# A four-layer transformer beside a two-of-eight expert layer: phases written out, tail and gathers reordered, new slot tables

## The chip, the cores and the metric

The kernel runs on one core of a Trainium2 chip. The metric is the time of one execution on the device in microseconds (us). Five engines work beside each other, each through its own list of instructions in order: PE (TensorE, matrix products), DVE (VectorE), ACT (ScalarE), POOL (GpSimd) and SP (SyncE, which here only starts transfers). They meet at semaphores: an instruction waits until a counter has reached a value, and what stands behind it in the same list waits too.

## The reference, cut to what matters

The input x has 2 rows of 1024 positions and 128 features. After one layer normalisation it goes through two things, whose results are both added to x:

```python
xn = layernorm(x)
x + attn(xn) + moe(xn)

# attn: 4 layers, 16 heads of 8 features, hidden width 512
mask = -inf above the diagonal, slope[h] * (k - q) below it
for i in range(4):
    x = x + mha(layer_norm(x, ln1), mask)      # softmax(q k / sqrt(8) + mask) v, then out_proj
    x = x + gelu(layer_norm(x, ln2) @ ffn1 + b1) @ ffn2 + b2
return layer_norm(x, final)

# moe: 8 experts of width 512; each position takes its two best, weighted by a softmax of the two logits
```

A softmax does not depend on which number is subtracted from a row of scores before the exponential, as long as the same number is used in numerator and sum.

## The kernel before, in words

Everything is written engine by engine, with all waits by hand. The work of attention is cut into 32 passes (U in the code): a pass is one layer, one row and a group of four heads. Four passes are a phase; there are eight phases, alternating between the two rows: an even phase does the attention of row 0 and the dense work of row 1, an odd one the other way round. Phase 0 is written out ("first"), phases 1 to 6 are three turns of a hardware loop (`Fori`) whose body holds an odd phase and an even one, and phase 7 is written out again ("last"). Behind phase 7 comes a tail (`END`) that finishes row 1: output projection, feed-forward and last normalisation, for two halves c = 0 and 1 of 512 positions.

In a pass each engine does two things at once. For the next pass, PE computes scores (L967, with the mask added by L972) and DVE takes their maxima (L1216, L1223); there are 40 such steps, through two banks of PSUM. For the present pass, PE computes the transposed scores with the maximum subtracted (L984, L990) in 24 slots, ACT takes the exponentials (L797), and PE multiplies by the values (L1002). POOL splits each maximum into three bf16 parts (`max_parts`, L601 to L608), PE transposes them (`turn`, L879), ACT copies them out (L766), and SP puts them as three rows into the operand of the transposed scores (`minus_max`, L455), for two halves of the positions. So `turn` must follow the end of a pass's maxima, and slot 0 or 8 of the pass follows `turn`.

Between the slots PE does the dense work, all through bank 7: output projection (`wo`, L938), normalised rows transposed (`ln1`, `ln2`, L887), hidden layer (`h`, L907 for attention's, L911 for the experts'), second layer (`y`, L924, L927), and `q`, `k`, `v` of the next layer (L948, L952). The order is written in tables, `PLANS`: `pace` says how many of the 40 score steps stand in each half slot (48 for each of four passes), `contents` gives the slot (0 to 95 in the phase) at which PE does a piece and the half slot at which another engine takes it out, and the rest are slots for ACT's gelu and splits and for DVE's statistics, reciprocals, normalisation and final step. A `turn` for half 1 takes the pass to which its slot belongs (slots 0 to 23 are pass 0, and so on).

The experts' rows are scattered by POOL in phase 0 (L614, 32 indirect transfers), and gathered back in phase 7 (`gather`, L641, 32 indirect transfers: 16 at the end of pass 0 and 16 at the end of pass 1, before the reciprocal roots `rstd_of`, L572, that stand behind them). In pass 2 POOL then weights and adds them (`combine`, L650, L654); DVE's `final` (L1210) needs these sums.

`wait_apart` (L373) is a wait in an instruction of its own, made so by a count on a semaphore that nobody reads (`passed`, L376).

In the tail before, PE's order is `wo` 0, `ln2` 0, four `h` of half 0, `wo` 1, `ln2` 1, four `h` of half 1, `y` 0, `y` 1. DVE copies the hidden layer out of PSUM (L1138) and computes the reciprocals and the normalisation for `wo` 1 (L1194, L1199) after the four `h` of half 0.

Of the kernel before, what the change touches and what calls it, by code (L numbers as in the profile page):

```python
# [57 lines left out]
def first_pass():  # L58

    steps = []  # L60
    for i in range(TB):
        for c in range(1 + i // 4):
# [12 lines left out]
        pace=("011111011111011111011111011111011101021111011111",  # L75
              "011111011111011112011110011111010111111111011021",
              "011111011111011112001111011111011111101111101111",
              "011101111001111100013101000043011111110111101111"),
        contents=(
# [6 lines left out]
        gelu=(14, 23, 59, 83), stats2=(1, 17), stats1=(19, 36),  # L86
        recip=(87, 5), norm=(94, 13), hi=(32, 45), mid=(36, 49), final=(72, 75)),
    "odd": dict(
        pace=("020111011110111111011110111110111111000311101111",
              "000103211020111101101001211111110111002111011102",  # L90
              "001021012011100121011110000430111101110120110012",
              "011101012111011011101110005310001011101111110102"),
        contents=(
# [11 lines left out]
        gelu=(13, 26, 59, 83), stats2=(2, 14), stats1=(21, 36),  # L105
        recip=(88, 8), norm=(95, 13), hi=(32, 45), mid=(36, 49), final=(73, 73)),
    "even": dict(
        pace=("011110111110101111101111111112011002011111012110",
              "000002321200111101111011110211010111101101111111",
              "001011112111011111111012011010011111210110011103",  # L110
              "101101220011101210010010100431111100110111011102"),
        contents=(
# [10 lines left out]
        gelu=(13, 27, 62, 85), stats2=(1, 14), stats1=(19, 36),  # L123
# [100 lines left out]
def build(nc, x, cA, rA, cB, moe1, moe2, router_w, rb, fin, ident, identb, iota, m1, m2, route, kcon, qcon, out):  # L224
    with ExitStack() as ctx:
# [147 lines left out]
        def wait_apart(eng, semaphore, value):  # L373

            eng.wait_ge(semaphore, value)
            eng.sem_inc(passed, 1)  # L376
# [1106 lines left out]
```

## Time and profile before

| | |
|---|---|
| median of 3 runs | 1548.06 us (1546.43 to 1549.83) |
| the profiled execution's own time | 1548.17 us |
| its span, first to last instruction | 1546.4 us |
| executed instructions in the profile | 35310 |
| PE busy | 1272.3 us (82%) |
| DVE busy | 997.0 us (64%) |
| ACT busy | 873.0 us (56%) |
| POOL busy | 379.2 us (25%) |
| mean granted clock of TensorE | 0.921 |

Times inside the profile are counted from the first instruction of the span. The profiled execution lies 1.8 us outside its span. "Idle before, releaser" in a row is the time for which the engine did nothing before that instruction and what ended it; "issue" is a gap for which the profile shows no wait. PEld is the weight load that goes ahead of a product. A granted clock of 1.0 is 2.4 GHz, 0.5 is 1.2 GHz.

### The profile page before, as it was taken

Reading aid. Unit: us, or ns where it says so; the run is one execution under the profiler, and the core shown is the slowest. Engines: PE = TensorE matmul, PEld = TensorE weight load, DVE = VectorE, ACT = ScalarE, POOL = GpSimd, SP = SyncE. Lnnn points to the kernel's source line nnn. Section 1 sums busy time; section 2 is a strip of 40 time slices with the busy share of each in tenths; the row PEclk is TensorE's granted clock in tenths of the full one; section 3 lists DMA queues with packets and bytes.
Section 4 is the critical chain, followed back from the end, with each engine's and each line's share of the span. In section 5 each row is a group of like instructions: output and inputs, shape, how many; then the busy total and the mean of one; then the engine's idle time right before and its main releaser. Section 6 shows DMA issues by size and latency. Waiting matters only on the chain.

```text
span 1546.4 us, 35310 instructions
## 1 busy us (share of the span) xinstructions
PE 1272.3 (82%) x12316; PEld 647.1 (42%) x12316; DVE 997.0 (64%) x2120; ACT 873.0 (56%) x1107; POOL 379.2 (25%) x569
## 2 busy tenths in 40 slices
PE   3688788899888887889888897889988898976854
PEld 2333344345444443444444443444544444433323
DVE  5787666666666775666665776657666676745724
ACT  2056556666566664656655665566565666653740
POOL 4044503132031201222122110312203210424501
PEclk9589889999999998999998999999998999988986
DMA  8212414123230312313232131303313041201010
GB/s 247 65 45 86 173 38 128 31 73 116 73 117 19 117 50 65 111 33 115 80 103 66 59 107 54 112 18 114 108 58 97 20 140 36 88 30 48 18 48 15
DMA packets 108919, 120.64 MB, mean 78 GB/s; under 512 B 12097, under 2 KB 95169, under 8 KB 108737
## 3 DMA queue, kind: packets, MB, share of 16 engines
q1 hardware_dynamic: 100288, 90.38, 18.7%
q0 software_dynamic: 8448, 27.88, 6.0%
q8 instruction: 109, 1.79, 0.5%
q14 instruction: 74, 0.60, 0.1%
HBM read 78.63 MB, written 40.89 MB: 77 GB/s over the span
## 4 chain that ended last, share of the span: by engine, by line
PE 52%; DVE 15%; issue 14%; POOL 10%; ACT 6%; DMA 1%; POOLq 0%; DVEq 0%; ACTq 0%; SPq 0%
PE PS L1002 13%; PE PS L967 12%; DVE mx L1216 10%; PE PS L984 5%; PE PS L924 4%; PE PS L927 3%; PE PS L907 3%; PE PS L911 3%; ACT PR L797 2%; POOL xs L614 2%; POOL both L641 2%; PE PS L948 2%; PE PS L972 2%; PE PS L990 2%; PE PS L952 1%
## 5 line engine op out<-in xcount | busy, mean ns | idle before, releaser
L1216 DVE TENSOR_REDUCE mx<-PS 128x1 f32<-128x512 f32 (+3 forms) x1280 | 768.3, 633 | 351.2 <-PE PS L972 231.2
L797 ACT ACTIVATE PR<-PS 128x1024 f32<-128x1024 f32 (+3 forms) x768 | 607.4, 810 | 499.2 <-PE PS L990 311.4
L967 PE MATMUL PS<-Kop,Qop 64*128 64x512 bf16 (+3 forms) x1536 | 438.4, 346 | 140.1 <-DVE mx L1216 135.8
L984 PE MATMUL PS<-Qop,Kop 64*128 64x512 bf16 (+3 forms) x1536 | 349.0, 338 | 16.3 <-ACT PR L797 8.4
L1002 PE MATMUL PS<-PR,vbuf 128*32 128x512 f32 (+3 forms) x3072 | 342.4, 519 | 0.6 <-ACT PR L797 0.4
L967 PEld LDWEIGHTS PS<-Kop,Qop 64*128 64x128 bf16 x1536 | 130.9, 94 | 467.8 <-DVE mx L1216 371.4
L972 PE MATMUL PS<-idb,mk 64*128 64x64 bf16 x2048 | 192.0, 195 | 0.0
L972 PEld LDWEIGHTS PS<-idb,mk 64*128 64x128 bf16 x2048 | 163.4, 98 | 45.1 <-issue 7.2
L990 PE MATMUL PS<-idb,mk 64*128 64x64 bf16 x2048 | 168.3, 194 | 4.7 <-issue 4.7
L601 POOL CAST mp<-negm 128x16 bf16<-128x16 f32 x64 | 14.9, 234 | 555.2 <-DVE negm L1223 555.2
L990 PEld LDWEIGHTS PS<-idb,mk 64*128 64x128 bf16 x2048 | 136.3, 97 | 33.7 <-issue 8.3
L984 PEld LDWEIGHTS PS<-Qop,Kop 64*128 64x128 bf16 x1536 | 106.0, 95 | 104.7 <-ACT PR L797 58.0
L572 POOL TENSOR_TENSOR rstd<-ve,mhalf 128x4 f32<-128x4 f32 x40 | 41.1, 1027 | 240.7 <-DVE ve L1118 240.4
L1002 PEld LDWEIGHTS PS<-PR,vbuf 128*32 128x32 f32 x3072 | 61.6, 109 | 64.9 <-issue 34.6
L907 PE MATMUL PS<-xnT,wF 128*128 128x512 f32 x128 | 76.0, 687 | 11.9 <-ACT xnT L757 9.3
L924 PE MATMUL PS<-wF,hb 128*128 128x128 f32 x512 | 73.2, 294 | 4.5 <-ACT hb L779 2.9
L924 PEld LDWEIGHTS PS<-wF,hb 128*128 128x128 f32 x512 | 64.1, 200 | 13.3 <-issue 6.6
L577 POOL TENSOR_TENSOR x<-x,parts 128x1024 f32<-128x1024 f32 x16 | 34.1, 2128 | 131.1 <-ACT parts L784 131.1
L779 ACT ACTIVATE hb<-hb 128x2048 f32<-128x2048 f32 x26 | 49.7, 1910 | 18.9 <-DVE hb L1138 12.5
L927 PE MATMUL PS<-w2G,hb 128*128 128x128 f32 x320 | 54.0, 322 | 0.4 <-issue 0.4
L590 POOL TENSOR_TENSOR xr<-xr,wR 128x512 f32<-128x512 f32 x28 | 35.6, 1271 | 76.4 <-DVE xc L1130 76.4
L766 ACT ACTIVATE mrow<-PS 12x512 bf16<-12x512 bf16 x64 | 36.8, 575 | 27.5 <-PE PS L879 27.0
(104 smaller groups left out, 1117.3 us busy)
## 6 DMA issues: line engine op xcount, KB each, us to landing
Qop<-qst SPq DMA_DIRECT2D x64, 256.0 KB, 2.8
Kop<-kst SPq DMA_DIRECT2D x64, 256.0 KB, 3.3
kst<-parts SPq DMA_DIRECT2D x32, 256.0 KB, 2.9
qst<-parts SPq DMA_DIRECT2D x16, 384.0 KB, 2.5
kst<-parts SPq DMA_DIRECT2D x32, 128.0 KB, 2.5
qst<-parts SPq DMA_DIRECT2D x16, 256.0 KB, 2.7
Qop<-mrow SPq DMA_DIRECT2D x256, 3.0 KB
onum<-osb SPq DMA_DIRECT2D x256, 16.0 KB
```

Of the source, the lines that this page charges most:

```text
L779: act.activation(hb[:, HBUF[chunk], :, :], hb[:, HBUF[chunk], :, :], ACT.Gelu).then_inc(S["s_gelu"], 1)
L797: act.activation(PR[:, c % 4, :, 0:n], PS[:, 2 * (c % 2):2 * (c % 2) + 2, 0:n], ACT.Exp)\
L907: last = pe.matmul(PS[:, bank, :], wF[:, P * f:P * f + P], xnT[:, row, 512 * c:512 * c + 512], start=True, stop=True)
L911: last = pe.matmul(PS[:, bank, P * m:P * m + P], w1G[:, f, P * m:P * m + P], xGT[:, P * f:P * f + P], start=True, stop=True)
L924: last = pe.matmul(PS[:, bank, P * j:P * j + P], hb[:, HBUF[k], m, P * j:P * j + P], wF[:, F + P * m:F + P * m + P], start=(m == 0), stop= ...
L927: last = pe.matmul(PS[:, bank, P * j:P * j + P], hb[:, HBUF[k], j, P * m:P * m + P], w2G[:, j, P * m:P * m + P], start=(m == 0), stop=(m = ...
L967: last = pe.matmul(PS[:, 5 + k % 2, n * e:n * e + n], Qop[r, par, a, P * i:P * i + P], Kop[r, kb, a, 512 * c:512 * c + n], start=True, sto ...
L972: last = pe.matmul(PS[:, 5 + k % 2, at:at + ROWS], mk1[r, side, :], idb[r, r], start=False, stop=side == 1)
L984: last = pe.matmul(PS[:, 2 * (c % 2) + j, 0:n], Kop[r, kb, a, P * kt:P * kt + P], Qop[r, par, a, q0:q0 + n], start=True, stop=not DIAG[t])
L990: last = pe.matmul(PS[:, 2 * (c % 2) + j, ROWS * side:ROWS * side + ROWS], mk2[r, side, :], idb[r, r], start=False, stop=side == 1)
L1002: last = pe.matmul(PS[32 * h:32 * h + 32, 4, q0 - 512 * qh:512], vbuf[:, par, kt, h, :], PR[:, 2 * (t % 2) + h // 2, h % 2, 0:n], start=t ...
L1216: dve.tensor_reduce(mx[:, par, i, 2 * heads[0] + j:2 * heads[-1] + j + 1:2, c], PS[:, 5 + k % 2, 0:n * len(heads)].rearrange("p (h n) -> p ...
```

## The change

- The loop over the middle six phases becomes a Python loop: the six are written out one behind the other, with constants for semaphore values and addresses.
- `wait_apart` loses its count, so that its wait can go into the instruction that follows.
- In phase 7 the 32 gathers are issued in four groups of eight: at the very end of passes 0 and 1, and twice in pass 2 (behind the first `values`, and behind `max_parts`). `combine` moves from pass 2 to pass 3, behind the last `max_parts`.
- In the tail PE's order is `wo` 0, `ln2` 0, `h` of half 0, `wo` 1, `y` 0, `ln2` 1, `h` of half 1, `y` 1. ACT copies the hidden layer out of PSUM instead of DVE, and DVE's reciprocals and normalisation for `wo` 1 come right behind the normalised rows of half 0.
- The slot tables of all four kinds of phase are replaced.

```diff
         def wait_apart(eng, semaphore, value):
             eng.wait_ge(semaphore, value)
-            eng.sem_inc(passed, 1)
...
-            with sp.Fori(0, L - 1, 1) as l:
+            for l in range(L - 1):
                 phase(2 * l + 1, 1, l, l + 1, odd_base(l), ODD_PLAN)
                 phase(2 * l + 2, 0, l, l + 1, even_base(l), EVEN_PLAN)
...
 END = [((), k, c) for k, c in
-       [("wo", 0), ("ln2", 0)] + [("h", (0, f)) for f in range(FT)]
-       + [("wo", 1), ("ln2", 1)] + [("h", (1, f)) for f in range(FT)] + [("y", 0), ("y", 1)]]
+       [("wo", 0), ("ln2", 0)] + [("h", (0, f)) for f in range(FT)] + [("wo", 1), ("y", 0), ("ln2", 1)]
+       + [("h", (1, f)) for f in range(FT)] + [("y", 1)]]
-END_AFTER = (0, 1) + (2,) * 4 + (2, 7) + (8,) * 4 + (12, 12)
+END_AFTER = (0, 1, 2, 2, 2, 2, 6, 6, 8, 9, 9, 9, 9, 13)
...
 # POOL, phase()
+                    if q is None and j == 2:
+                        gather(TB, NT)
+                    if q is None and j == 3:
+                        wait_apart(pool, S["c_both"], 16 * RANKS)
+                        for half in range(4):
+                            combine(half // 2, half % 2)
...
-                    if q is None and j == 0:
-                        wait_apart(pool, S["c_ys"], 16 * (TILES // GROUP))
-                    if q is None and j < 2:
-                        gather(16 * j, 16 * j + 16)
                     if q is None and j == 2:
-                        wait_apart(pool, S["c_both"], 16 * RANKS)
-                        for half in range(4):
-                            combine(half // 2, half % 2)
+                        gather(NT + TB, 2 * NT)
...
+                    if q is None and j == 0:
+                        wait_apart(pool, S["c_ys"], 16 * (TILES // GROUP))
+                        gather(0, TB)
+                    if q is None and j == 1:
+                        gather(NT, NT + TB)
...
 # ACT, tail
             for c in range(2):
                 n = number(END, "ln2", c)
                 norm_out(base + n, 2, L - 1, 1, c, END_BANK[n])
+                for f in range(FT):
+                    n = number(END, "h", (c, f))
+                    h_out(base + n, c, f, 1, END_BANK[n])
                 gelu(c, base + number(END, "h", (c, 3)) + 1)
...
 # DVE, tail (before: in the order of END, with the reciprocals ahead of wo 1)
+            end_out("wo", 0)
+            ln_stats(8 * L + 4, 1, 0, xr)
+            ln_apply(8 * L + 4, 1, 0, xr, xc)
+            reciprocals(L - 1, 1, 1)
+            normalise(L - 1, 1, 1)
+            end_out("wo", 1)
...
 # of the tables: the pieces that are named below, as (slot of PE, piece, which, half slot of the copy)
-  first: ((50,), 'turn2', 1, 101)
+  first: ((47,), 'turn2', 1, 95)
-  even:  ((26,), 'turn1', 1, 53), ((50,), 'turn2', 1, 100), ((71,), 'turn3', 1, 142)
+  even:  ((24,), 'turn1', 1, 50), ((47,), 'turn2', 1, 98),  ((73,), 'turn3', 1, 146)
-  last:  ((61,), 'turn2', 0, 122), ((74,), 'turn3', 1, 148); recip=(88, 5), norm=(93, 13), final=(73, 75)
+  last:  ((58,), 'turn2', 0, 116), ((71,), 'turn3', 1, 142); recip=(90, 3), norm=(92, 11), final=(83, 92)
```

## Rows read from the trace of the kernel before

**Rows 1.** Windows: stretch, its length, busy time of each engine, granted clock, DMA.

```profile
601.80:791.00 189.20, 165.14 (x1591) 87.13 (x1589) 121.39 (x244) 113.33 (x143) 41.18 (x63) 0.95 0.27 82
1322.40:1482.60 160.20, 128.56 (x1289) 57.44 (x1289) 90.42 (x192) 96.78 (x126) 64.17 (x85) 0.89 0.13 39
```

**Rows 2.** Timeline of PE around the start of an odd phase: start, length, instruction.

```profile
240.42 1.06 PE L1002 MATMUL PS<-PR,vbuf 128*32 128x512 f32 x8
243.55 1.16 PE L938 MATMUL PS<-wB,x 128*128 128x128 f32 x8
...
594.16 1.07 PE L1002 MATMUL PS<-PR,vbuf 128*32 128x512 f32 x8
598.68 0.61 PE L984 MATMUL PS<-Qop,Kop 64*128 64x512 bf16 x2 [3.45 <-issue]
...
604.79 1.30 PE L938 MATMUL PS<-wB,x 128*128 128x128 f32 x8
...
958.98 1.07 PE L1002 MATMUL PS<-PR,vbuf 128*32 128x512 f32 x8
...
970.31 1.16 PE L938 MATMUL PS<-wB,x 128*128 128x128 f32 x8
```

**Rows 3.** The page's queues that load instructions: packets, MB, share of 16 engines.

```profile
q8 instruction: 109, 1.79, 0.5%
q14 instruction: 74, 0.60, 0.1%
```

**Rows 4.** Timeline of POOL in phase 7: first and last of the first 16 gathers.

```profile
1338.18 1.04 POOL L641 DMA_INDIRECT both<-ys,slot  x1 [0.53 <-issue]
...
1357.17 0.94 POOL L641 DMA_INDIRECT both<-ys,slot  x1 [0.30 <-issue]
```

**Rows 5.** Timeline of DVE in phase 7, behind the roots that follow the gathers.

```profile
1359.22 0.60 DVE L1130 TENSOR_SCALAR xc<-xr,mv,rstd 128x128 f32<-128x128 f32 x2 [4.68 <-POOL rstd L572]
...
1416.26 0.60 DVE L1130 TENSOR_SCALAR xc<-xr,mv,rstd 128x128 f32<-128x128 f32 x2 [8.75 <-POOL rstd L572]
```

**Rows 6.** Timeline of PE and ACT: where a transposition or a split waits for POOL.

```profile
166.22 0.59 PE L879 MATMUL PS<-idb,mp 128*12 128x128 bf16 x4 [6.90 <-POOL mp L608]
...
168.27 1.06 ACT L789 ACTIVATE parts<-x 128x1024 bf16<-128x1024 f32 x1 [8.86 <-POOL x L577]
...
1464.01 0.39 PE L879 MATMUL PS<-idb,mp 128*12 128x128 bf16 x4 [1.73 <-POOL mp L608]
```

**Rows 7.** Timeline of all engines in the tail.

```profile
1490.38 1.11 DVE L1130 TENSOR_SCALAR xc<-xr,mv,rstd 128x128 f32<-128x128 f32 x4 [1.13 <-POOL rstd L572]
...
1493.49 1.28 ACT L779 ACT_TABLE_LOAD   x1
...
1493.53 6.61 PE L907 MATMUL PS<-xnT,wF 128*128 128x512 f32 x8 [0.87 <-ACT xnT L757]
...
1500.85 0.93 DVE L1194 RECIPROCAL den<-den 64x128 f32<-64x128 f32 x1
1500.96 1.91 ACT L779 ACTIVATE hb<-hb 128x2048 f32<-128x2048 f32 x1 [6.19 <-DVE hb L1138]
...
1506.94 0.69 DVE L1199 TENSOR_TENSOR x<-x 128x512 f32<-128x512 f32 x1 [5.16 <-DMA x<-orec]
...
1507.69 2.07 PE L938 MATMUL PS<-wB,x 128*128 128x128 f32 x8 [7.55 <-DVE x L1199]
...
1514.43 1.11 PE L887 MATMUL PS<-idf,xc 128*128 128x128 f32 x4 [4.67 <-DVE xc L1130]
...
1516.41 5.42 PE L907 MATMUL PS<-xnT,wF 128*128 128x512 f32 x8 [0.87 <-ACT xnT L757]
...
1522.67 7.41 PE L924 MATMUL PS<-wF,hb 128*128 128x128 f32 x64 [0.84 <-DVE hb L1138]
...
1533.48 0.69 DVE L1157 TENSOR_TENSOR xr<-PS,xr 128x512 f32<-128x512 f32 x1 [0.18 <-DVE xc L1210]
```

**Rows 8.** The waits of their own, L376: engine, count, ns min/median/max, first and last.

```profile
L376 PEldq EVENT_SEMAPHORE  x104: 51/51/51, 17.6 to 1524.6; - x104
```

More of the change, by code:

```diff
@@ L74 @@
     "first": dict(
[L75 to L78, printed above, removed]
+        pace=("011111011111001211101111101111011101002111111111",
+              "011111011111011121011110011111010111111010111031",
+              "010211001111111100111110112111011111101111101111",
+              "011101111001111200003101000133011111110112010012"),
@@ L79 @@
         contents=(
[6 rows of a table removed]
-        gelu=(14, 23, 59, 83), stats2=(1, 17), stats1=(19, 36),
-        recip=(87, 5), norm=(94, 13), hi=(32, 45), mid=(36, 49), final=(72, 75)),
[6 rows of a table added]
+        gelu=(13, 22, 60, 83), stats2=(2, 18), stats1=(19, 36),
+        recip=(88, 3), norm=(94, 15), hi=(32, 46), mid=(36, 49), final=(71, 72)),
     "odd": dict(
[L89 to L92, printed above, removed]
+        pace=("020111011110111111011110111111011111000311101111",
+              "010010332110001111000201211011020110021020112011",
+              "000120211101100101121110001430110111000220000212",
+              "011001111211101001111000153110010111101110101300"),
@@ L93 @@
         contents=(
[4 rows of a table removed]
[4 rows of a table added]
             ((27,), 'ln1', 0, 55), ((28,), 'q', 0, 56), ((29,), 'k', 0, 59), ((30,), 'v', 0, 60),
[6 rows of a table removed]
-        gelu=(13, 26, 59, 83), stats2=(2, 14), stats1=(21, 36),
-        recip=(88, 8), norm=(95, 13), hi=(32, 45), mid=(36, 49), final=(73, 73)),
[6 rows of a table added]
+        gelu=(13, 27, 60, 84), stats2=(2, 14), stats1=(21, 37),
+        recip=(90, 8), norm=(95, 13), hi=(31, 42), mid=(32, 54), final=(64, 71)),
     "even": dict(
[L108 to L111, printed above, removed]
+        pace=("201011111101010120102011111102202001011111012110",
+              "000002321201111100011111110202010111110102021101",
+              "002111110101202111101102011010011101220100111031",
+              "101012012011110111010010011314011101011010111102"),
@@ L112 @@
         contents=(
[10 rows of a table removed]
-        gelu=(13, 27, 62, 85), stats2=(1, 14), stats1=(19, 36),
-        recip=(87, 3), norm=(94, 10), hi=(32, 44), mid=(36, 54), final=(73, 76)),
[10 rows of a table added]
+        gelu=(14, 29, 56, 84), stats2=(1, 14), stats1=(19, 36),
+        recip=(88, 2), norm=(94, 9), hi=(35, 47), mid=(35, 49), final=(73, 81)),
     "last": dict(
-        pace=("011111011111011111011111011111011111011111011111",
-              "000003311110101101121011111011110111110111011111",
-              "011111101111001111021111011011011120102020111111",
+        pace=("011110111200111112011110011111011110001210120112",
+              "000003311111001101121101110102101101111111011111",
+              "011111021110001110102121011011011201012020111111",
@@ L129 @@
               "000000000000000000000000000000000000000000000000"),
         contents=(
[6 rows of a table removed]
-        gelu=(14, 23, 59, 83), stats2=(1, 14), stats1=(19, 36),
-        recip=(88, 5), norm=(93, 13), hi=(35, 47), mid=(36, 49), final=(73, 75)),
[6 rows of a table added]
+        gelu=(13, 25, 62, 83), stats2=(1, 14), stats1=(19, 39),
+        recip=(90, 3), norm=(92, 11), hi=(33, 47), mid=(34, 49), final=(83, 92)),
 }
@@ L735, in _ @@
             phase(0, 0, None, 0, len(START), FIRST_PLAN)
-            with pool.Fori(0, L - 1, 1) as l:
+            for l in range(L - 1):
                 phase(2 * l + 1, 1, l, l + 1, odd_base(l), ODD_PLAN)
@@ L766, in turn_out, with h_out @@
                 act.activation(mrow[:, par, 512 * half:512 * half + 512], TURN, ACT.Copy).then_inc(S["s_taken"], 1)
-            def h_out(n, k, f, b):
+            def h_out(n, k, f, b, bank=7):
                 act.wait_ge(S["s_full"], n + 1)
-                act.activation(hb[:, HBUF[k], f, :], MISC, ACT.Identity, bias=wF[:, 2 * F + f:2 * F + f + 1])\
+                act.activation(hb[:, HBUF[k], f, :], PS[:, bank, :], ACT.Identity, bias=wF[:, 2 * F + f:2 * F + f + 1])\
                     .then_inc(S["s_taken"], 1)
@@ L854, in _ @@
             phase(0, 0, None, 0, len(START), FIRST_PLAN)
-            with act.Fori(0, L - 1, 1) as l:
+            for l in range(L - 1):
                 phase(2 * l + 1, 1, l, l + 1, odd_base(l), ODD_PLAN)
@@ L1076, in _ @@
             phase(0, 0, None, 0, len(START), FIRST_PLAN)
-            with pe.Fori(0, L - 1, 1) as l:
+            for l in range(L - 1):
                 phase(2 * l + 1, 1, l, l + 1, odd_base(l), ODD_PLAN)
@@ L1369, in _ @@
             phase(0, 0, None, 0, len(START), FIRST_PLAN)
-            with dve.Fori(0, L - 1, 1) as l:
+            for l in range(L - 1):
                 phase(2 * l + 1, 1, l, l + 1, odd_base(l), ODD_PLAN)
@@ L1374, in _, with end_out @@
             base = odd_base(L - 1) + len(LAST_PLAN)
-            for n, (_, kind, which) in enumerate(END):
-                if (kind, which) == ("wo", 1):
-                    reciprocals(L - 1, 1, 1)
-                    normalise(L - 1, 1, 1)
-                out_of_bank(base + n, kind, which, 0, 8 * L - 2, 1, 1, END_BANK[n])
-                if kind == "wo":
-                    dve.wait_ge(S["s_taken"], base + n + 1)
-                    ln_stats(8 * L + 4 + which, 1, which, xr)
-                    ln_apply(8 * L + 4 + which, 1, which, xr, xc)
-                if kind == "y":
-                    dve.wait_ge(S["s_taken"], base + n + 1)
-                    ln_stats(8 * L + 6 + which, 1, which, xr)
-                    ln_apply(8 * L + 6 + which, 1, which, xr, xc)
-                    final(1, which, 8 * L + 6 + which)
+            def end_out(kind, c):
+                n = number(END, kind, c)
+                out_of_bank(base + n, kind, c, 0, 8 * L - 2, 1, 1, END_BANK[n])
+                dve.wait_ge(S["s_taken"], base + n + 1)
+            end_out("wo", 0)
[4 more added lines that the diff above has]
+            end_out("wo", 1)
+            ln_stats(8 * L + 5, 1, 1, xr)
+            ln_apply(8 * L + 5, 1, 1, xr, xc)
+            for c in range(2):
+                end_out("y", c)
+                ln_stats(8 * L + 6 + c, 1, c, xr)
+                ln_apply(8 * L + 6 + c, 1, c, xr, xc)
+                final(1, c, 8 * L + 6 + c)
 def bf16_bits(a):
```

64 rows, old and new, of the table contents are left out of this document.

## The prediction

> **What bounds the kernel now.** I read the windows by phase first, then the chain of waits, then the timelines where that chain leaves PE. In a middle phase PE is busy 165.14 of 189.20 us, DVE 121.39, ACT 113.33 [rows 1]: the reader is to see that the phases hang on PE, and that about 24 us of each are left in which PE does nothing. Those 24 us are the most that any reordering of slots can win there, per phase. In phase 7 PE is busy only 128.56 of 160.20 us, at a granted clock of 0.89 instead of 0.95 [rows 1], so that is where something other than PE ends last. The chain names three such places: gaps called "issue" twice at the loop's end, POOL's gathers in phase 7, and a tail in which one engine works at a time.
>
> **The loop.** At the start of an odd phase PE goes from a value product of the phase before (L1002) to the output projection (L938). On entry into the loop, where nothing is jumped, this takes 243.55 - 240.42 = 3.13 us. At the first jump back it takes 604.79 - 594.16 = 10.63 us, at the second 970.31 - 958.98 = 11.33 us; inside lies a gap of 3.45 us called "issue" and more like it [rows 2]. Written out there is no jump: 7.50 + 8.20 = 15.7 us go, all on PE, and PE sets the end of these phases. Bounds: 12 (a part of the gap is spent on waits that come anyway) to 20 (the pass behind each jump is some us longer than its like).
>
> What does three times the code cost? The two queues that load instructions moved 1.79 + 0.60 MB [rows 3] for 35310 executed instructions: 68 bytes for each one executed, so the loop's body was loaded anew in each of its turns already. Straight code loads no more than that; I cost it at nothing. If that cover is gone, a phase would show gaps called "issue" of the kind above.
>
> The Trainium skill (Advanced Engine Details and Errata, Control Flow Timing) gives a compare-and-branch about 108 ns. By that the two jumps would be worth 0.2 us, and the sum below would end 15.5 us later. The rows disagree by a factor of seventy; the skill's page Runtime: NRT & Kernel Launch (Instruction fetch mechanics) says why they may: a jump to code that isn't held makes the engine wait for its transfer.
>
> **Waits in the instructions.** PE has 104 of these separate waits at 51 ns, 5.3 us in all [rows 8]; most are passed while a product still runs or while the wait itself lasts. Bounds 0 and 8 (5.3 and something for the other engines); I take 2. No wait is added by this edit, so nothing new is queued.
>
> **The gathers in phase 7.** A group of 16 gathers takes 1357.17 + 0.94 - 1338.18 = 19.9 us, 1.27 us from start to start [rows 4]; there are two. In passes 0 and 1 DVE stands still for 4.68 and 8.75 us until POOL has done the root that is queued behind them [rows 5], and with DVE the score steps of PE. After the change the gathers stand behind the roots. Of 8.75 us I take all, since PE has no other work then. Of 4.68 us I take 3, since other pieces of PE lie beside it (bounds 0 and 4.7). What is late next: eight gathers, 10 us, now stand before `max_parts` of half 0 in pass 2, whose `turn` moves forward from slot 61 to 58; I take 1 us lost (bounds 0 and 3). The lower clock behind the two stalls should go with them: 2 us (bounds 0 and 5, from 0.89 against 0.95 over the phase).
>
> **`combine` and the last `turn`.** In pass 2 `combine` held POOL while PE waited 1.73 us for the last `turn` [rows 6]. Two edits remove this wait: `combine` now follows that `max_parts`, and the table puts this `turn` at slot 71, which by the code is still pass 2. It then takes the maxima of pass 2, which have long been there, and waits for nothing. (The number subtracted is another one; the softmax isn't changed by that.) I take 1.7 us (bounds 0 and 4). `combine` then runs beside the last pass, which has no score steps; DVE's `final` for row 0 moves behind it and ends near the moment at which the tail needs DVE: 0, bounds 0 and 2 lost.
>
> Phase 7 in sum: 8.75 + 3 + 2 + 1.7 - 1 = 14.5 us.
>
> **The tail** [rows 7]. Half 0's rows are normalised at 1490.38 + 1.11 = 1491.49. The reciprocals start at 1500.85, behind four copies of `h`; now they start at 1491.49, 9.36 us earlier, and the normalisation behind their two transfers at 1506.94 - 9.36 = 1497.6. PE is through the four `h` at 1493.53 + 6.61 = 1500.14 and can do `wo` 1 at once instead of at 1507.69. Its normalised rows are there 7.55 us earlier, so `ln2` 1 could start at 1514.43 - 7.55 = 1506.9. But `y` 0 now stands before it and needs the gelu: ACT ends the last copy at about 1500.9 (0.8 behind `h`, as DVE did: its gelu began at 1500.96), loads a table (1.28, so far hidden beside DVE's copies, now in the way), takes 1.91, and `y` 0 runs from 1504.1 to 1507.8 (half of 7.41). `ln2` 1 starts there, 6.6 us earlier than before. From `ln2` 1 to the end of `h` it takes 1516.41 + 5.42 - 1514.43 = 7.40 as before: 1515.2. Copy, gelu and `y` 1: 0.8 + 1.91 + 3.7, 1521.6. Then DVE takes `y` 1 at once, where it took it at 1533.48, behind `final` of `y` 0: 11.9 us earlier. All that follows is unchanged. If `y` 0 falls on the half clock (as `wo` 1 did, 2.07 us against 1.16 in [rows 2]) 3.7 us come back. I take 10 (bounds 4 and 13).
>
> **The slot tables.** Most moves are by a slot or less. Where the trace shows the wait, I name it: in phase 0 `turn2` moves from slot 50 to 47, so that it takes pass 1's maxima and the 6.90 us for which PE waited there go; but ACT was held at its own split until 168.27 by the same POOL [rows 6], and PE needs its exponentials within two slots: 1 us (bounds 0 and 3). In each even phase `turn1` moves to slot 24, the first of its pass, and `turn3` from 71, where by the code it took pass 2's maxima, to 73, where it must wait for `max_parts`. Behind a waiting `turn` stands all of PE. The nearest row for such a wait is 1.73 us [rows 6]; I take 1 us for each, 6 us lost in three phases (bounds 0 and 14). The other moves I can't price from rows: at most the 24 us a phase, at worst as much. The pace strings put more steps together (2s and 3s) and leave more half slots free where DVE has pieces to take out. I take 9 us won, 6% of what is idle in the six middle phases (bounds 30 won, 20 lost). Net of the tables: 1 - 6 + 9 = 4 won.
>
> **Sum.** 15.7 + 2 + 14.5 + 10 + 4 = 46.2 us off the profiled execution's 1548.17 (span 1546.4 and 1.8 around it), which is 0.1 from the median of 1548.06: 1502 us.
>
> **Rivals.**
> 1. The gap at the jump isn't the jump's, and straight code keeps it, or a like one, at the seams of the phases: 1502 + 15.7 = 1518. For it: the profile calls the gap "issue" and shows no wait in it. Against it: the entry into the loop runs the same odd phase without the gap [rows 2]. The figure of 108 ns in the Trainium skill (Advanced Engine Details and Errata, Control Flow Timing) would speak for it.
> 2. The covers fill up: the stalls of phase 7 and the tail turn into others (half clock in the tail, POOL's ten us before `max_parts`, the transfers of the last denominators) and win 10 instead of 24.5, and the tables nothing: 1548.2 - 15.7 - 2 - 10 = 1520. For it: in the tail each wait is followed closely by another [rows 7].
> 3. The tables win more: a fifth of the idle 24 us in six phases, 29 us instead of 4: 1477. For it: phases that hang on PE and still leave 24 us.
> 4. Slower than before: a `turn` or a split queued ahead of POOL's part in each of the six middle phases. The row shows what one such place can cost, 6.90 us of PE with 8.86 us of ACT beside it [rows 6]; at 9 us a phase, six phases lose 54 us against the 46: 1556. It decides from 7.7 us a phase. Against it: the moves that I can follow give 2 us a phase.
>
> **How the numbers follow.** My forecast 0.55 (its own range 1486 to 1515), rivals 1 and 2 together 0.21, rival 3 0.16, rival 4 with everything that ends above 1551 0.06, an end within 0.2% of before (about 3 us, what a measurement of this kernel can tell from no change) 0.02. The range 1478 to 1522 takes in rivals 1 and 2 and nearly reaches rival 3. So faster 0.92, same 0.02, slower 0.06.
>
> **What would show it.** At the seams between phases PE's way from L1002 to L938 should be 3.1 to 3.5 us everywhere, and no "issue" gap over 2 us on PE. In phase 7 no wait of DVE for the root over 2 us, and the phase some 145 us long. In the tail `wo` 1 right behind `h`, with DVE taking `y` 1 as soon as PE has it, and 10 us less from the first projection to the end. In the even phases, waits of PE for POOL's L608 tell what the moved `turn`s cost. The prediction is wrong if the middle phases change by more than 5 us each apart from the seams: then the tables, which I price least well, decide.

## The result and the profile after

The changed kernel takes 1504.57 us (median of 4 runs, 1494.97 to 1508.89), the kernel before 1548.94 beside it: 44.4 us between the medians. The ratio is 0.9695, 95% interval 0.9657 to 0.9733, which is 47 us (41 to 53). Forecast were 1502 us and 46.2 us. The profiled execution of the kernel after is the fastest of its four, 1494.97 us, so its profile shows 53.2 us less than that of before, not 44.4; the clocks of the four runs, 0.937, 0.930, 0.923 and 0.919, fall as their times rise. Of the runs below, one each of e5, e7 and e10 (1552.63, 1523.09 and 1523.39 us) lies over 1.5% above the fastest of its kernel; the medians and ranges given count it, and without it the medians are 1533.37, 1507.15 and 1502.75 us.

The page of the kernel after: span, PE's busy time (share, instructions), the queues that load instructions, the chain by engine.

```profile
span 1493.2 us, 30375 instructions
PE 1258.0 (84%) x12316; PEld 632.6 (42%) x12316; DVE 990.1 (66%) x2112; ACT 880.3 (59%) x1115; POOL 379.4 (25%) x569
...
q8 instruction: 97, 1.59, 0.5%
q14 instruction: 42, 0.34, 0.1%
...
PE 59%; DVE 21%; POOL 6%; issue 6%; ACT 6%; DMA 1%; SPq 1%; POOLq 0%; DVEq 0%; ACTq 0%
```

Instruction loads went down, from 2.39 MB [rows 3] to 1.93 MB, per executed instruction from 68 to 64 bytes (64 too in e1 below, 1.99 MB for 30984, where only the loop is written out): code written out three times was loaded no more than the loop's body was. And no gap called "issue" longer than 1.75 us is left on PE; before there were four of 2.07 to 3.63 us, all at the two jumps.

Where the 53.2 us went is read best by phases. Each phase is counted here from its first exponential to the first one of the next; the first stretch is all before phase 0, the tail is counted from the start of phase 7's last exponential.

| us | ahead | 0 | 1 | 2 | 3 | 4 | 5 | 6 | 7 | tail |
|---|---|---|---|---|---|---|---|---|---|---|
| before | 85.6 | 156.4 | 185.5 | 174.3 | 189.2 | 176.3 | 185.6 | 169.4 | 160.3 | 63.7 |
| after | 85.7 | 160.8 | 188.1 | 163.8 | 184.3 | 164.7 | 185.3 | 161.3 | 145.9 | 53.3 |
| difference | +0.1 | +4.4 | +2.6 | -10.5 | -4.9 | -11.6 | -0.3 | -8.1 | -14.4 | -10.4 |

**The seams.** Windows of the last pass of phases 2, 4 and 6 in the kernel before (stretch, length, busy time of PE, PEld, DVE, ACT, POOL, granted clock, DMA). Behind the first two stands a jump back, behind the third none.

```profile
554.80:601.77 46.97, 37.58 (x390) 20.83 (x384) 28.13 (x49) 25.31 (x31) 2.57 (x11) 0.93 0.16 47
920.77:967.29 46.52, 36.11 (x390) 19.70 (x384) 28.05 (x49) 25.31 (x32) 2.57 (x11) 0.96 0.16 48
1282.68:1322.37 39.69, 35.51 (x392) 19.63 (x384) 27.94 (x49) 25.31 (x32) 1.70 (x7) 1.00 0.17 51
```

The same pass is 7 us longer before a jump, with the same work in it. Most of that lies at its end, at the jump itself, as two more windows of the kernel before show: PE is busy 2.08 of 7.60 us, and the clock is 0.77 there and 0.50 in the 3 us behind.

```profile
594.20:601.80 7.60, 2.08 (x21) 0.60 (x21) 1.52 (x4) 0.52 (x2) 0.86 (x4) 0.77 0.23 77
601.80:604.80 3.00, 3.00 (x27) 0.89 (x25) 0.76 (x2) 1.36 (x2) 0.00 (x0) 0.50 0.02 5
```

In the kernel after, the ways of PE that took 10.63 and 11.33 us across a jump [rows 2] are as short as the one on entry, 3.13 us, as the timeline of PE shows at the first of them:

```profile
596.96 1.07 PE L1009 MATMUL PS<-PR,vbuf 128*32 128x512 f32 x8
...
600.09 1.16 PE L945 MATMUL PS<-wB,x 128*128 128x128 f32 x8
```

**A middle phase and phase 7.** Windows of the kernel after for the two stretches of [rows 1].

```profile
598.40:782.70 184.30, 162.58 (x1602) 83.99 (x1601) 121.51 (x247) 114.16 (x142) 42.63 (x69) 0.94 0.27 83
1294.00:1439.90 145.90, 120.41 (x1290) 54.56 (x1290) 89.73 (x189) 97.00 (x126) 63.91 (x85) 0.98 0.16 44
```

Phase 3 still has 21.7 us without PE, where it had 24. Phase 7 lost 14.3 us, and its clock rose from 0.89 to 0.98. POOL's timeline shows why: the root comes first and the eight gathers behind it, and half 0's maxima stand behind those.

```profile
1335.84 1.02 POOL L571 TENSOR_TENSOR rstd<-ve,mhalf 128x4 f32<-128x4 f32 x1 [4.40 <-DVE ve L1125]
1337.03 1.04 POOL L640 DMA_INDIRECT both<-ys,slot  x1 [0.18 <-issue]
...
1345.90 0.95 POOL L640 DMA_INDIRECT both<-ys,slot  x1 [0.31 <-issue]
```

DVE waited 4.68 and 8.75 us for these roots [rows 5]. The two longest such waits of phase 7 are now, in the timeline of DVE:

```profile
1301.26 0.60 DVE L1137 TENSOR_SCALAR xc<-xr,mv,rstd 128x128 f32<-128x128 f32 x2 [0.21 <-POOL rstd L571]
...
1376.01 0.60 DVE L1137 TENSOR_SCALAR xc<-xr,mv,rstd 128x128 f32<-128x128 f32 x2 [0.70 <-POOL rstd L571]
```

In pass 2 eight gathers now stand ahead of `max_parts`, and PE waits there; the last `turn`, at 1417.0, waits for nothing.

```profile
1398.72 0.39 PE L886 MATMUL PS<-idb,mp 128*12 128x128 bf16 x4 [1.59 <-POOL mp L607]
```

**The tail.** Timeline of the kernel after, in order of time; the rows answer to [rows 7].

```profile
1447.45 1.11 DVE L1137 TENSOR_SCALAR xc<-xr,mv,rstd 128x128 f32<-128x128 f32 x4 [1.17 <-POOL rstd L571]
1448.48 0.94 DVE L1201 RECIPROCAL den<-den 64x128 f32<-64x128 f32 x1
...
1457.09 1.28 ACT L783 ACT_TABLE_LOAD   x1
1457.22 1.13 PE L945 MATMUL PS<-wB,x 128*128 128x128 f32 x8 [0.87 <-ACT hb L774]
1458.39 1.91 ACT L783 ACTIVATE hb<-hb 128x2048 f32<-128x2048 f32 x1
1460.35 5.47 PE L931 MATMUL PS<-wF,hb 128*128 128x128 f32 x32 [2.00 <-ACT hb L783]
1466.76 0.63 PE L894 MATMUL PS<-idf,xc 128*128 128x128 f32 x4 [0.94 <-DVE xr L1164]
...
1480.40 0.69 DVE L1164 TENSOR_TENSOR xr<-PS,xr 128x512 f32<-128x512 f32 x1 [7.84 <-PE PS L931]
```

From the end of the first normalisation (1448.56) it takes 31.8 us until DVE takes `y` 1, where it took 1533.48 - 1491.49 = 42.0 before: 10.2 us less. The reciprocals start at once, `wo` 1 stands right behind the last `h`, and the table load is now in the way, all as forecast. One thing was not: `y` 0 takes 5.47 us and not 3.7. The windows of `y` 0 and `y` 1 show why, in the granted clock, 0.69 and 1.00: PE ran a good part of `y` 0 at 1.2 GHz.

```profile
1460.35:1465.80 5.45, 5.45 (x32) 5.27 (x32) 1.41 (x7) 0.00 (x0) 2.29 (x2) 0.69 0.00 0
1476.43:1480.30 3.87, 3.84 (x32) 3.65 (x32) 0.00 (x0) 0.00 (x0) 0.00 (x0) 1.00 0.00 0
```

### The profile page after: what moved, and what is told of

It is laid out like the page before. It is cut to its first block, busy times and chain, and to the rows that moved or that the text cites. A ratio compares the mean times of both kernels' runs of the same rounds, so it can differ in the third digit from the quotient of the medians.

```text
span 1493.2 us, 30375 instructions
## 1 busy us (share of the span) xinstructions
PE 1258.0 (84%) x12316; PEld 632.6 (42%) x12316; DVE 990.1 (66%) x2112; ACT 880.3 (59%) x1115; POOL 379.4 (25%) x569
## 3 DMA queue, kind: packets, MB, share of 16 engines
q8 instruction: 97, 1.59, 0.5%
## 4 chain that ended last, share of the span: by engine, by line
PE 59%; DVE 21%; POOL 6%; issue 6%; ACT 6%; DMA 1%; SPq 1%; POOLq 0%; DVEq 0%; ACTq 0%
PE PS L1009 16%; DVE mx L1223 14%; PE PS L974 12%; PE PS L991 6%; PE PS L931 5%; PE PS L914 3%; PE PS L918 3%; PE PS L955 3%; PE PS L934 3%; PE PS L979 2%; PE PS L997 2%; ACT PR L801 2%; POOL w1G L624 1%; DVE st L1114 1%; POOL w2G L633 1%
## 5 line engine op out<-in xcount | busy, mean ns | idle before, releaser
L979 PE MATMUL PS<-idb,mk 64*128 64x64 bf16 x2048 | 191.0, 195 | 0.0
L979 PEld LDWEIGHTS PS<-idb,mk 64*128 64x128 bf16 x2048 | 162.6, 98 | 50.5 <-issue 8.7
L997 PE MATMUL PS<-idb,mk 64*128 64x64 bf16 x2048 | 173.7, 194 | 0.0
L914 PE MATMUL PS<-xnT,wF 128*128 128x512 f32 x128 | 73.8, 669 | 14.3 <-ACT hb L774 8.7
L774 ACT ACTIVATE hb<-PS,wF 128x512 f32<-128x512 f32 x64 | 44.0, 688 | 26.2 <-PE PS L914 25.7
```

Of the source, the lines that this page charges most:

```text
L914: last = pe.matmul(PS[:, bank, :], wF[:, P * f:P * f + P], xnT[:, row, 512 * c:512 * c + 512], start=True, stop=True)
L979: last = pe.matmul(PS[:, 5 + k % 2, at:at + ROWS], mk1[r, side, :], idb[r, r], start=False, stop=side == 1)
L997: last = pe.matmul(PS[:, 2 * (c % 2) + j, ROWS * side:ROWS * side + ROWS], mk2[r, side, :], idb[r, r], start=False, stop=side == 1)
```

## The experiments

Each ratio is to the kernel before, run beside it on the same chip in five rounds: e1 to e4 on one chip, e5, e6, e7 and e9 on a second, e8, e10, e12 and e13 on a third. Kernels of different chips are compared by their ratios.

**One part alone.** First the loop, written out on all five engines, and nothing else.

```
-            with pe.Fori(0, L - 1, 1) as l:
+            for l in range(L - 1):
```

> The kernel before with its middle six phases written out, nothing else changed. Theory (each taken jump back costs PE 7.5 to 8.2 us): 15.7 us less, 1533 us, ratio 0.990; on PE the way from L1002 to L938 is 3.1 to 3.5 us at every start of an odd phase, and the gaps called issue are gone. Rival (the gap is not the jump's): the gaps stay, 1548 us, ratio 1.000. Rival (straight code that is three times longer makes engines wait for instructions): gaps called issue at other places, ratio above 0.995.

Measured: 1523.47 us, 0.9837 (0.9796 to 0.9878), about 25 us (19 to 32). More than forecast, and no gap called "issue" over 1.5 us is left on PE. Its windows for the last passes of phases 2 and 4 show where the most of it comes from:

```profile
555.47:595.01 39.54, 35.56 (x393) 19.41 (x391) 28.02 (x49) 25.37 (x31) 1.70 (x7) 1.00 0.17 50
907.05:946.65 39.60, 35.58 (x394) 19.42 (x393) 28.04 (x49) 25.38 (x32) 1.70 (x7) 1.00 0.17 49
```

Both are as short as the pass without a jump was before: 7.4 and 6.9 us less, and the clock is 1.00 instead of 0.93 and 0.96. The first pass behind each jump went from 53.2 and 51.1 to 49.0 and 48.8 us, another 4.2 and 2.3. That makes 20.8 us in four passes for two jumps, and the 7.50 and 8.20 us of [rows 2] are in it: that way of PE spans the end of one pass and the start of the next. What e1 won beyond that isn't at the seams: the first pass of phase 4, ahead of which nothing is jumped, took 48.5 us here and 52.6 before.

A first pass of some 53 us comes without a jump too, as shown below. But in the five kernels that keep a loop (before, e2 to e5) all nine first passes behind a jump took 51.1 to 53.2 us, and the six of odd phases without one 48.8 to 51.1 us.

Then a loop of two turns and the last turn written out, so that one of the two jumps is gone.

```
-            with pe.Fori(0, L - 1, 1) as l:
+            with pe.Fori(0, L - 2, 1) as l:
                 phase(2 * l + 1, 1, l, l + 1, odd_base(l), ODD_PLAN)
                 phase(2 * l + 2, 0, l, l + 1, even_base(l), EVEN_PLAN)
+            for l in range(L - 2, L - 1):
+                phase(2 * l + 1, 1, l, l + 1, odd_base(l), ODD_PLAN)
+                phase(2 * l + 2, 0, l, l + 1, even_base(l), EVEN_PLAN)
```

> The kernel before with a loop of two turns and the third written out behind it: one taken jump instead of two. Theory: half of the gain, some 8 us, 1540 us, ratio 0.995, one gap of the old size and none at the place of the second. If the gain of writing out lay in constants instead of registers, it would be a third of that of the whole and would not be tied to the jump: ratio 0.997.

Measured: 1538.02 us, 0.9933 (0.991 to 0.9957), 10.4 us. The jump that is left keeps its 46.90 us for phase 2's last pass, and in PE's timeline the gaps called "issue":

```profile
597.23 0.61 PE L993 MATMUL PS<-Qop,Kop 64*128 64x512 bf16 x2 [3.91 <-issue]
...
600.53 0.29 PE L999 MATMUL PS<-idb,mk 64*128 64x64 bf16 x4 [2.69 <-issue]
```

The seam without a jump has 39.69 us. So the gap belongs to the jump, and rival 1 falls. The ratio doesn't exclude that constants instead of registers won it, since a third of the gain of e1 would be 0.9946; the profile does: passes 1 and 2 of the even phases take 46.2 and 30.9 us inside the loop, 46.3 and 30.9 in the turn written out.

The new order of the tail alone (END, its banks, and the ACT and DVE parts):

```
-       [("wo", 0), ("ln2", 0)] + [("h", (0, f)) for f in range(FT)]
-       + [("wo", 1), ("ln2", 1)] + [("h", (1, f)) for f in range(FT)] + [("y", 0), ("y", 1)]]
+       [("wo", 0), ("ln2", 0)] + [("h", (0, f)) for f in range(FT)] + [("wo", 1), ("y", 0), ("ln2", 1)]
+       + [("h", (1, f)) for f in range(FT)] + [("y", 1)]]
```

> The kernel before with the new tail alone (order of PE, copies of h on ACT, reciprocals early). Theory: 10 us less, 1538 us, ratio 0.9935; wo 1 right behind h of half 0, y 1 taken by DVE at once. Rival (other waits or the half clock take its place): 4 us or less, ratio above 0.997.

Measured: 1535.36 us, 0.9904 (0.9873 to 0.9936), about 15 us. In its profile the tail is 50.5 us long, 13.2 less than before: the upper bound of the forecast (13).

The new order of the gathers and of `combine` alone:

```
+                    if q is None and j == 2:
+                        gather(TB, NT)
...
-                    if q is None and j < 2:
-                        gather(16 * j, 16 * j + 16)
...
+                    if q is None and j == 0:
+                        wait_apart(pool, S["c_ys"], 16 * (TILES // GROUP))
+                        gather(0, TB)
```

> The kernel before with the new places of gathers and combine alone, old tables. Theory: 12 to 15 us less, 1535 us, ratio 0.991; DVE's waits for the root in phase 7 (4.68 and 8.75 us) below 2 us. Rival (the covers fill up): 5 us or less, ratio above 0.9965, with PE waiting for max_parts behind a group of gathers.

Measured: 1535.55 us, 0.9913 (0.9883 to 0.9944), 13.5 us. Phase 7 is 149.4 us long in its profile, 10.9 less, and DVE's longest wait for a root is 0.68 us.

The new slot tables alone, all four (a line of the even one stands for them):

```
-            ((43,), 'k', 1, 88), ((45,), 'v', 1, 90), ((50,), 'turn2', 1, 100), ((62,), 'turn2', 0, 124),
+            ((43,), 'k', 1, 88), ((45,), 'v', 1, 90), ((47,), 'turn2', 1, 98), ((65,), 'turn2', 0, 130),
...
```

> The kernel before with the new slot tables alone (the loop, the tail and the gathers as before). Theory of the prediction: 4 us less net, ratio 0.997. Rival from the sum of the parts (writing out 25, tail 15, gathers 13.5 us less, 53 together, where the whole is 47 less): the tables win nothing or lose some 6 us, ratio 1.000 to 1.004.

Measured: 1533.41 us (1527.56 to 1552.63), 0.9896 (0.9868 to 0.9924), 16 us, four times what I gave them. By phases, against the profile of before: phase 0 +7.6; phases 2, 4, 6 -4.3, -4.7, -6.2; phase 3 -3.8; phase 7 -4.9. In every even phase pass 1 takes 42.9 us instead of 46.2, and pass 2 29.8 instead of 30.9.

**The kernel after with one part put back.** With the counting increments back at the separate waits:

```
             eng.wait_ge(semaphore, value)
+            eng.sem_inc(passed, 1)
```

> The changed kernel with the count on an unread semaphore put back behind each separate wait. Theory: 2 us slower than the changed kernel, that is a ratio of 0.971 to before against 0.9695. If these waits cost nothing: 0.9695. If they cost all of their 51 ns on PE and something on the other engines (8 us): 0.975.

Measured: 1501.15 us, 0.9678 (0.964 to 0.9716). No dearer than the kernel after. That excludes the 8 us of the upper bound (0.975), but the interval holds 0.971 as well as 0.9695: whether the waits cost 2 us or nothing isn't decided.

With all four old tables:

```
-            ((43,), 'k', 1, 88), ((45,), 'v', 1, 90), ((47,), 'turn2', 1, 98), ((65,), 'turn2', 0, 130),
+            ((43,), 'k', 1, 88), ((45,), 'v', 1, 90), ((50,), 'turn2', 1, 100), ((62,), 'turn2', 0, 124),
...
```

> The changed kernel with the old slot tables: written out, no counts, new gathers and tail. If the tables won 4 us: 1508 us, ratio 0.972. If the parts add up (53 us less): 1494 us, ratio 0.966, faster than the changed kernel.

Measured: 1511.43 us (1499.02 to 1523.09), 0.9709 (0.9659 to 0.9759). The tables that won 16 us in the looped kernel are worth no more than a few here. The forecast of 0.972 lies well inside the interval; 0.966, by which the parts would add up, lies at its edge.

With the old table of phase 0 alone, since by the profiles the new one makes that phase some 4 us longer:

```
-            ((47,), 'turn2', 1, 95), ((61,), 'turn2', 0, 124), ((74,), 'turn3', 1, 148), ((75,), 'xt', 3, 150),
+            ((50,), 'turn2', 1, 101), ((61,), 'turn2', 0, 123), ((74,), 'turn3', 1, 148), ((75,), 'xt', 3, 150),
...
```

> The changed kernel with the old table for phase 0 alone. In the traces phase 0 became longer with its new table (first exponential to first exponential of phase 1: 156.4 us before, 160.8 after). If that is the table's doing, this runs 3 to 5 us under the changed kernel, ratio 0.967; if it is the run's clock, 0.9695.

Measured: 1502.7 us, 0.9682 (0.9641 to 0.9723). Phase 0 is 157.8 us in its profile, 3.0 less than after; the total doesn't tell the two apart.

With the old tables of phase 0 and the odd phases (to the edit of the last one comes):

```
-            ((32, 32, 32, 34), 'y', 1, 70), ((36,), 'turn1', 0, 76), ((41,), 'ln1', 1, 82), ((41,), 'q', 1, 82),
+            ((33, 33, 35, 36), 'y', 1, 72), ((38,), 'turn1', 0, 78), ((41,), 'ln1', 1, 82), ((41,), 'q', 1, 82),
...
```

> The kernel after with the tables of phase 0 and of the odd phases as before, and the even phases' and the last one's new; nothing is left out. Theory: what the new tables win in the written-out kernel lies in the even phases (4 us each by the profiles of passes 1 and 2); so this one is not slower than the kernel after: 1495 to 1502, ratio 0.967. Rival: the new odd table wins 2 us a phase, and this one is 4 to 8 us slower than that, ratio 0.972.

Measured: 1500.97 us, 0.969 (0.9662 to 0.9718). Not slower, as the theory had it; the rival, a gain in the odd table, isn't seen. Phase 0 took 162.6 us this time with the old table, so that its 4 us aren't the table's alone. What goes with the table is pass 1 of phase 0: 42.5 us in all four profiles with the new one, 39.7 to 39.8 in nine of ten with the old one.

With the old tables and the counts, which leaves the written-out loop, the tail and the gathers (to the edit of the old tables comes):

```
             eng.wait_ge(semaphore, value)
+            eng.sem_inc(passed, 1)
```

> The kernel before with loop written out, new tail and new gathers, but old tables and with the counting increment kept at the waits; nothing is left out. With the new tables the counts made no difference (1501.2 against 1502 to 1505). Theory: they make none with the old tables either, so it ends with the kernel after on old tables, 1511 (1499 to 1523), ratio 0.971. Rival: the new tables were fitted to the faster waits, and the old tables show what the counts cost: a ratio above 0.975.

Measured: 1504.22 us (1499.06 to 1523.39), 0.9733 (0.9689 to 0.9777). No cost of the counts is seen with the old tables either (e7 has 0.9709), but the interval reaches past the rival's 0.975.

**What the clock does in the odd phases.** The first pass of an odd phase ends in one of two ways, with the same instructions: in the written-out kernels in 48.6 to 50.0 us or in 52.3 to 54.3. In the kernel after, phase 1 shows the second, phase 3 the first. Windows of the kernel after around the second output projection (`wo` 1) of both phases: two stretches of phase 1, then the same of phase 3.

```profile
272.00:274.00 2.00, 0.59 (x4) 0.62 (x5) 1.29 (x2) 1.98 (x2) 0.00 (x0) 0.90 1.00 318
274.00:281.00 7.00, 6.06 (x30) 5.01 (x29) 2.54 (x10) 1.80 (x3) 0.00 (x0) 0.54 0.28 90
624.00:626.00 2.00, 1.13 (x8) 0.97 (x8) 1.26 (x3) 1.98 (x2) 0.00 (x0) 1.00 0.69 211
626.00:633.00 7.00, 6.22 (x60) 4.19 (x60) 4.43 (x17) 3.76 (x5) 1.05 (x1) 1.00 0.24 81
```

In phase 1 the DMA engines are full (share 1.00, where phase 3 has 0.69), DVE waits for the denominators `x<-orec`, PE waits behind DVE, and then the clock is at half: PE gets 30 products done in the 7 us in which phase 3 does 60. The timeline of both phases (PE's row calls its gap "issue", but in both it starts 0.11 us behind the end of DVE's row):

```profile
272.61 0.69 DVE L1206 TENSOR_TENSOR x<-x 128x512 f32<-128x512 f32 x1 [1.56 <-DMA x<-orec]
273.41 1.85 PE L945 MATMUL PS<-wB,x 128*128 128x128 f32 x8 [1.75 <-issue]
...
623.35 0.69 DVE L1206 TENSOR_TENSOR x<-x 128x512 f32<-128x512 f32 x1 [0.39 <-DMA x<-orec]
624.15 1.13 PE L945 MATMUL PS<-wB,x 128*128 128x128 f32 x8 [0.58 <-issue]
```

The seven kernels that are written out and have these transfers in the same place (the kernel after, e1, e6 to e10) bear this out: of their 21 first passes nine had the fall, and in all nine PE had waited 1.01 to 2.54 us ahead of `wo` 1. In eleven of the other twelve it had waited 0.05 to 0.91 us, in one 1.40.

The transfers that fill the engines there are eight gathers of expert weights that POOL issues from 12 to 22 us into the pass. So I moved these to its end, behind the last `add_bias`:

```
-                    if j == 0 and f is not None and q is not None:
-                        g = group_of(2 if b == 1 else 3, b, f)
-                        weights_1(g, base)
-                        weights_2(g, None)
...
                         if f is None:
                             scatter(16, 32)
+                    if j == 0 and f is not None and q is not None:
+                        g = group_of(2 if b == 1 else 3, b, f)
+                        weights_1(g, base)
+                        weights_2(g, None)
```

> The kernel after, with the eight weight gathers of POOL in pass 0 of the middle phases (w1G, w2G) issued behind the last add_bias of that pass, some 20 us later; nothing is left out. In the first odd phase of the kernel after, the DMA engines were full (share 1.00) while wo 1 waited 1.75 us, the clock fell to half for 6.8 us behind it, and the phase's pass 0 took some 53 us; in the second odd phase the share was 0.69, nothing waited, and it took some 49. Theory A: the gathers' packets delay the row x<-orec that wo 1 needs, and this decides the fall. Then all three odd phases have pass 0 at about 49 us, and the time falls by 4 us for each of the one to two falls in a run: 1495 to 1500 us, ratio to the kernel before 0.966. Rival B: the fall has another cause; the odd phases still show both outcomes, and the time stays at 1501 to 1506, ratio 0.970. Rival C: the gathers now come late for h of unit 2 (slot 54), PE waits there, and the time rises by more than 5 us, ratio above 0.973.

Measured: 1559.19 us, 1.0065 (1.0044 to 1.0087): all of the change's gain is given away. Theory A was right on these passes and wrong on the time; rival C was right on the time alone. Windows of the first pass of phases 1, 3 and 5, in the kernel after and then in this one:

```profile
246.60:299.70 53.10, 45.27 (x402) 22.82 (x397) 33.98 (x84) 31.67 (x41) 15.19 (x22) 0.94 0.33 94
598.40:647.60 49.20, 42.56 (x404) 20.50 (x400) 33.80 (x85) 31.62 (x40) 15.53 (x23) 1.00 0.33 100
947.40:997.40 50.00, 42.55 (x402) 20.48 (x399) 33.79 (x85) 31.60 (x40) 15.54 (x23) 1.00 0.32 97
```

```profile
245.10:293.70 48.60, 42.51 (x402) 20.48 (x398) 33.62 (x84) 31.60 (x40) 7.38 (x13) 1.00 0.18 55
615.00:663.70 48.70, 42.62 (x404) 20.59 (x400) 33.81 (x85) 31.63 (x41) 7.66 (x14) 1.00 0.18 52
987.30:1036.00 48.70, 42.63 (x404) 20.60 (x400) 33.80 (x85) 31.64 (x41) 7.66 (x14) 1.00 0.17 53
```

All three are short, at a clock of 1.00, and DVE finds its denominators there in each. But the next pass is 8.5 to 12.2 us longer than in the kernel after in the odd phases and 10.9 to 13.7 in the even ones. Not for `h` of unit 2, as rival C had it, but for a `turn`: the eight gathers now stand ahead of the next `max_parts` in POOL's queue, and PE waits for that, 10.88 us in each odd phase and 9.2 in each even one. POOL's first gather and the first row behind the last, then PE's wait, from the timeline of this kernel:

```profile
296.73 1.04 POOL L624 DMA_INDIRECT w1G<-in_moe,wsel  x1 [0.28 <-POOL wsel L621]
...
306.54 0.22 POOL L600 CAST mp<-negm 128x16 bf16<-128x16 f32 x1
...
307.68 0.59 PE L886 MATMUL PS<-idb,mp 128*12 128x128 bf16 x4 [10.88 <-POOL mp L607]
```

The same with phase 0's old table:

```
-            ((47,), 'turn2', 1, 95), ((61,), 'turn2', 0, 124), ((74,), 'turn3', 1, 148), ((75,), 'xt', 3, 150),
+            ((50,), 'turn2', 1, 101), ((61,), 'turn2', 0, 123), ((74,), 'turn3', 1, 148), ((75,), 'xt', 3, 150),
...
```

> As the run with the late weight gathers, and the slot table of phase 0 as before; nothing is left out. By the profiles the old table of phase 0 takes 158 us where the new takes 162. Theory: both savings stand, 4 us from the table and what the late gathers give: 1491 to 1497 us, ratio 0.963. Rival: phase 0's difference is given back in phase 1, as the first pass of an odd phase waits for the same last rows, and it ends where the late gathers alone do.

Measured: 1555.78 us, 1.0058 (1.0031 to 1.0086). The expectation missed by 60 us for the same reason. Phase 0 took 156.6 us, and the first pass of the odd phases 48.7 us three times more.

No version here beats the kernel after by more than the runs can tell. Late gathers that stand behind the next `max_parts` as well were not tried.

## Why the prediction came out right

The time fell within 3 us of the forecast. Its terms were partly wrong, and their errors cancelled: alone, the loop, the tail and the tables each won more than forecast, 25, 15 and 16 us instead of 15.7, 10 and 4, and together the parts won 23 us less than their sum. That the total came out so near is luck; the mechanisms of the loop, of phase 7 and of the tail are not.

- **The loop: mechanism right, size somewhat too small.** Forecast 15.7 us, measured about 25 alone (19 to 32), of which 20.8 are in the passes around the two jumps, above the bound of 20. The term counted PE's way from one row to another across the jump, 7.50 and 8.20 us. Counted over both passes it is 11.6 and 9.2 us: most of what is added lies in the first pass behind the jump (2.7 and 0.8 us), where the bound of 20 had put it, the rest in the last pass ahead (1.4 and 0.2). A pass of the same work without a jump stood in the profile of before and would have given this. The Trainium skill gives a compare-and-branch about 108 ns (Advanced Engine Details and Errata, Control Flow Timing); the measurement is some hundred times that. What the Trainium skill's page Runtime: NRT & Kernel Launch (Instruction fetch mechanics) says of a jump to code that isn't held agrees with the gaps called "issue"; no run here shows the transfer itself.
- **The waits: 2 us forecast, none seen** (e6 against the kernel after, e10 against e7). The intervals are too wide to tell 2 us from none; that the 51 ns lie beside other waits is not shown.
- **Phase 7: 14.5 forecast, 14.4 in the profile of after,** 13.5 as a ratio alone. With the old tables (e10) phase 7 has 146.3 us, 14.0 less than before, so it is the order of POOL's work and not the table. The profiles with the new order scatter: with it phase 7 is 10.0 to 14.4 us shorter than before, and 14.4 is the most of them. The single terms are borne out too: no root is waited for over 0.7 us, the last `turn` waits for nothing, the eight gathers ahead of `max_parts` cost 1.59 us where I took 1, and the clock came back.
- **The tail: 10 forecast, 10.4 in the profile of after.** The 3.7 us that I kept as a bound for a `y` 0 on the half clock came in part: 1.6 us (5.47 instead of the 3.84 of `y` 1; in e9, whose tail is 50.5 us, `y` 0 took 3.84 too). Alone, e3 reached 13.2, with a `y` 0 of 3.81. In the seven other profiles with the new tail, that of the kernel after among them, `y` 0 took 5.44 to 5.47 us and the tail 52.9 to 53.6: the half clock there is the rule.
- **The tables: 4 net forecast; 16 alone, and nothing that the runs can tell in the written-out kernel** (by the ratios of e7 and the kernel after 2 us, give or take 10). The kernel after and e6 to e10 lie between 1500.97 and 1511.43 us with overlapping intervals, whichever tables and waits they have. The step that failed is the price of the moved `turn`s: I took 6 us lost in three even phases, and PE's waits for POOL's maxima show nothing of the kind. Over phases 1 to 7 in the kernel after (engine, line, for whom; total us, times, longest):

```profile
PE PS L886 <- POOL mp L607: 5.2, 8, 1.6
```

  In the even phases that is one wait of 0.64 us each. Instead the even table wins in passes 1 and 2, 4.4 us a phase, in the looped kernel and in the written-out one, and phase 0 loses some. The prediction named a sign against itself, middle phases that change by over 5 us each apart from the seams. One phase shows it clearly: phase 6, with no jump at either end, lost 8.1 us, 4.4 of them in these two passes. In phase 0 the 6.90 us wait of the `turn` did turn into another one, as I had it; PE now waits 6.66 us for the exponentials, behind ACT's split and POOL:

```profile
169.10 1.06 ACT L793 ACTIVATE parts<-x 128x1024 bf16<-128x1024 f32 x1 [6.93 <-POOL x L576]
...
170.91 0.39 PE L991 MATMUL PS<-Qop,Kop 64*128 64x256 bf16 x2 [6.66 <-ACT PR L801]
```

- **The rivals.** Rival 1 is refuted by e1 and e2. Rival 2 was half right in the tail only (the half clock). Rival 3 has some of the truth: alone, the tables win four times my value. Rival 4 named a mechanism that exists: in e12 a `turn` queued behind POOL costs 10.9 us three times and 9.2 us three times, where I priced it at 9. The change just doesn't do it.

**What stays open.** The four parts alone (loop, tail, gathers, tables) win 1.63, 0.96, 0.87 and 1.04%, in sum 4.5% or 70 us; together they win 3.05% or 47 us. Of the missing 23 us some 5 are phase 7, where by the profiles the tables win 4.9 us only as long as the gathers are in the way. The half widths of the four intervals make some 10 us of uncertainty on the sum (root of the sum of squares, 0.66%). The rest isn't explained. A part of it may be the clock of the odd phases: in the profiles of e1 and e10 none of the three first passes has the fall, in e7 all three do, and one fall costs 4 to 5 us. In the seven written-out kernels with early gathers it came 9 times in 21, in the two with late ones 0 times in 6. With the waits counted above, that supports the transfers as what tips it, but 0 in 6 isn't proof, and phase 5 of the kernel after waited 1.40 us and kept its clock.

## What to carry over

Price a taken jump by comparing a whole pass that has one with a whole pass of the same work that has none, not by the gap at the jump: the way across the two jumps showed 15.7 us of 20.8. In an engine's queue the order of short work that others wait for and long work that nobody needs yet decides; groups of eight gathers, some 1.26 us each, won 14 us in phase 7 when moved behind the roots, and other groups of eight lost 55 us in six phases when moved ahead of the maxima. And gains of single parts don't add up: try the last part on top of the others before it is kept for what it won alone.

## What the runs showed of the hardware

- A loop's jump back cost 9 to 12 us on this kernel (11.6 and 9.2 by the passes around the two, 10.4 by the time with one of them gone). At the first jump PE was busy 2.08 of 7.60 us, at a granted clock of 0.77, and ran the 3 us behind at 0.50.
- The same program ends a pass in some 49 or some 53 us, by whether TensorE is at its half clock (1.2 GHz; 0.54 over 7 us) behind the wait for `wo` 1; in the kernel after a wait of 1.75 us was followed by that, one of 1.40 us wasn't. This goes with the spread of the runs: 1494.97 us at a mean clock of 0.937, 1508.89 at 0.919.
- Separate waits on an engine's queue, 104 of 51 ns on PE alone [rows 8], could be put in or left out without a difference that five rounds can see; some 8 us would have shown.
